# A 4-bit FFN kernel: dequantization scales repeated over partitions by transfers, not by expander matmuls

## What is computed

```python
def dequant4bit(q, scale):                      # BLOCK = 64
    return (q.astype(jnp.float32) - 7.5) * jnp.repeat(scale, BLOCK, axis=1)
...
q_emb = relu(cond @ W3 + b3)                    # one vector per batch
v = (64 * x + sum over the 64 rows of x) * q_emb
x1 = relu(v @ W2 + b2)
w_up = dequant4bit(w_up_q, w_up_scale).T        # 512 x 2048
x2 = relu(x1 @ w_up + b_up + x1 @ w_up_lora_a @ w_up_lora_b)
w_down = dequant4bit(w_down_q, w_down_scale).T  # 2048 x 512
out = x + x2 @ w_down + b_down + x2 @ w_down_lora_a @ w_down_lora_b
```

## Time and profile before

| | us |
|---|---|
| median of 3 runs | 833.25 (833.24 to 834.16) |
| span of the profiled execution | 832.3 |
| PE busy | 811.9 (98%) |
| DVE busy | 302.3 (36%) |
| ACT busy | 239.4 (29%) |
| POOL busy | 21.4 (3%) |

### The profile page before, as it was taken

The page is one execution under the profiler, slowest core; times in us unless marked ns, Lnnn a source line. Parts: engine busy times, 40 slices in busy tenths (PEclk is TensorE's granted clock), DMA queues, the critical chain, the costliest instruction groups (busy, mean ns, idle before and its releaser), DMA issues.

```text
span 832.3 us, 9143 instructions
## 1 busy us (share of the span) xinstructions
PE 811.9 (98%) x3576; PEld 671.5 (81%) x3576; DVE 302.3 (36%) x450; ACT 239.4 (29%) x370; POOL 21.4 (3%) x16
## 2 busy tenths in 40 slices
PE   5799999999999999999999999999999999999998
PEld 4578888888888888888888888888888888888886
DVE  6888885322132331423223132332224222241111
ACT  3353442422232222322214222232223322132221
POOL 3411000000000000000000000000000000000000
PEclk9799999999999999999999999999999999999999
DMA  8910001500004000120004000040000300020001
GB/s 318 419 50 1 1 0 52 151 1 1 0 1 152 0 0 0 55 97 0 0 0 148 3 0 0 0 151 0 0 0 31 120 0 0 0 100 2 1 1 51
DMA packets 13697, 39.64 MB, mean 48 GB/s; under 512 B 1648, under 2 KB 1776, under 8 KB 11760
## 3 DMA queue, kind: packets, MB, share of 16 engines
q1 hardware_dynamic: 13392, 39.33, 13.5%
q10 hardware_dynamic: 288, 0.08, 0.0%
HBM read 31.01 MB, written 8.39 MB: 47 GB/s over the span
## 4 chain that ended last, share of the span: by engine, by line
PE 95%; DVE 4%; DMA 1%; issue 0%; ACT 0%; DVEq 0%; ACTq 0%
PE up_ps L488 15%; PE up_ps L489 15%; PE up_ps L490 15%; PE acc L488 14%; PE acc L489 14%; PE acc L490 14%; PE lora_ps L488 1%; PE scale_ps L488 1%; PE lora_ps L490 1%; PE scale_ps L490 1%; PE lora_ps L489 1%; PE scale_ps L489 1%; DMA biases<-in_biases 1%; DVE x_in L389 1%; DVE xm_lo L399 1%; DVE xm_hi L397 0%
## 5 line engine op out<-in xcount | busy, mean ns | idle before, releaser
L405 DVE TENSOR_TENSOR x_lo<-full,x_hi 128x512 fp32r<-128x512 f32 x160 | 110.5, 691 | 469.8 <-ACT x_hi L271 469.8
L269 ACT ACTIVATE full<-up_ps,biases 128x512 f32<-128x512 f32 x142 | 97.9, 689 | 508.9 <-PE up_ps L490 508.9
L488 PE MATMUL up_ps<-x_hi,w_up_hi 128*128 128x512 f32 x512 | 200.2, 391 | 0.7 <-DVE x_lo L405 0.7
L489 PE MATMUL up_ps<-x_lo,w_up_hi 128*128 128x512 f32 x512 | 200.1, 391 | 0.0
L490 PE MATMUL up_ps<-x_hi,w_up_lo 128*128 128x512 f32 x512 | 199.7, 390 | 0.0
L490 PE MATMUL acc<-x_hi,w_down_lo 128*128 128x512 f32 x512 | 199.2, 389 | 0.0
L489 PE MATMUL acc<-x_lo,w_down_hi 128*128 128x512 f32 x512 | 199.2, 389 | 0.0
L488 PE MATMUL acc<-x_hi,w_down_hi 128*128 128x512 f32 x512 | 199.2, 389 | 0.0
L488 PEld LDWEIGHTS up_ps<-x_hi,w_up_hi 128*128 128x128 f32 x512 | 96.4, 188 | 20.7 <-DVE x_lo L405 0.9
L490 PEld LDWEIGHTS up_ps<-x_hi,w_up_lo 128*128 128x128 f32 x512 | 96.5, 188 | 20.1
L489 PEld LDWEIGHTS up_ps<-x_lo,w_up_hi 128*128 128x128 f32 x512 | 96.6, 189 | 19.6
(11 more groups left out here) (68 smaller groups left out, 401.4 us busy)
## 6 DMA issues: line engine op xcount, KB each, us to landing
x_in<-in_x SPq DMA_DIRECT2D x32, 256.0 KB, 5.7
res<-in_x SPq DMA_DIRECT2D x8, 1024.0 KB, 6.8
out<-res SPq DMA_DIRECT2D x32, 256.0 KB, 2.7
codes_up<-in_q_up SPq DMA_DIRECT2D x3, 1024.0 KB, 18.7
codes_down<-in_q_down SPq DMA_DIRECT2D x3, 1024.0 KB, 21.1
raw_records<-in_records SPq DMA_DIRECT2D x3, 768.0 KB, 18.1
raw_w<-in_w SPq DMA_DIRECT2D x4, 256.0 KB, 7.9
raw_narrow<-in_narrow SPq DMA_DIRECT2D x1, 1024.0 KB, 11.4
```

The costliest lines, as they stand in the source:

```text
L269: act.activation(whole, source, ACT.Relu, bias=bias_col).then_inc(relu_done, 1)
L405: dve.tensor_tensor(lo, full[:, slot % FULL_SLOTS, :], hi.bitcast(F32), ALU.subtract).then_inc(act_split, 1)
L488: pe.matmul(dest, w_hi, a_hi, start=start, stop=False)
L489: pe.matmul(dest, w_hi, a_lo, start=False, stop=False)
```

## The change

The scales are no longer expanded by TensorE. A tile of 128 partitions (inputs) spans two groups of 64 inputs, so the host lays each table out as two rows of 16 x 512 elements (`s_up`, `s_down`), and SP loads each row with a source repeated over 64 partitions: `scale[0:64]` from row 0, `scale[64:128]` from row 1. For each of the five groups there are now six transfers: codes and two scale copies for up, and the same for down; the semaphore of the group is waited for at 96. The scale tables have the size of the codes and lie where the low parts go; the codes now lie where the high parts go.

`dequantize` reads codes and scales from SBUF and writes over the scales; the LoRA product is added in place, and `weight_high` and `weight_low` read from there. The scratch and the wait for it go. `expand` has one product left, into two banks `lora_ps` in turn. Of `records` only the LoRA part is left (`wide`, 16 x 128 per partition); it is loaded in one transfer, cast by one ACT copy, and split by one POOL instruction on 64 partitions, ahead of the last w2 tile's low part. `narrow` has two parts in place of four. The five record casts, the five record splits and the split of `scale_down` go. In front of group 0's loads stand narrow, wide and the last w2 tile.

The diff, cut to its core:

```diff
-        narrow_r = sb("narrow", [P, 3, D], F32R)
-        lora_up, scale_down, lora_down = narrow_r[:, 0, :], narrow_r[:, 1, :], narrow_r[:, 2, :]
-
-        codes_up = sb("codes_up", [P, NH, D], I32, over="w_up_lo")
-        codes_down = sb("codes_down", [P, NH, D], I32, over="w_down_lo")
-
-
-
-        REC = 3 * P
-        REC_SKIP = 4 * NH * (D - REC)
-        raw_narrow = sb("raw_narrow", [P, 4, D], F32, over="w_up_hi")
-        raw_records = sb("raw_records", [P, NH, REC], F32, over="w_up_hi", skip=REC_SKIP)
-        record = sb("record", [P, NH, REC], F32R, over="w_down_hi", skip=REC_SKIP)
-        raw_w2 = sb("raw_w2", [P, KD, D], F32, over="w_down_hi")
-        assert 4 * 4 * D <= REC_SKIP
-        weight = sb("weight", [P, 2, D], F32, over="res")
-        expand_up = sb("expand_up", [P, D], F32R, over="res", skip=2 * 4 * D)
+        narrow_r = sb("narrow", [P, 2, D], F32R)
+        lora_up, lora_down = narrow_r[:, 0, :], narrow_r[:, 1, :]
+        wide = sb("wide", [P, NH, P], F32R, over="res")
+
+        codes_up = sb("codes_up", [P, NH, D], I32, over="w_up_hi")
+        codes_down = sb("codes_down", [P, NH, D], I32, over="w_down_hi")
+
+        scale_up = sb("scale_up", [P, NH, D], F32, over="w_up_lo")
+        scale_down = sb("scale_down", [P, NH, D], F32, over="w_down_lo")
+        raw_wide = sb("raw_wide", [P, NH, P], F32, over="x1_hi")
+        raw_w2 = sb("raw_w2", [P, KD, D], F32, over="x1_lo")
+        raw_narrow = sb("raw_narrow", [P, 2, D], F32, over="x2_lo", skip=1024)
...
-        scale_ps = ctx.enter_context(nc.psum_tensor("scale_ps", [P, BANK], F32))
-        lora_ps = ctx.enter_context(nc.psum_tensor("lora_ps", [P, BANK], F32))
-        w2_ps = [up_ps[0], up_ps[1], scale_ps, lora_ps]
+        lora_ps = [ctx.enter_context(nc.psum_tensor(f"lora_ps{m}", [P, BANK], F32)) for m in range(2)]
+        w2_ps = up_ps + lora_ps
...
-        def scratch(e):
-            return like(e, weight[:, e % 2, :])
+        def whole(e):
+
+            return part_of(e, scale_up4, scale_down)
...
-            def load_group(g):
-                a, b = GROUPS[g]
-                sp.dma_start(raw_records[:, a:b, :], records[:, a:b, :]).then_inc(record_loaded[g], 16)
-
             def load_codes(g):
                 a, b = GROUPS[g]
-                sp.dma_start(codes_up[:, a:b, :], q_up[:, a:b, :]).then_inc(codes_loaded[g], 16)
-                sp.dma_start(codes_down[:, a:b, :], q_down[:, a:b, :]).then_inc(codes_loaded[g], 16)
+                for codes, q, scale, s in ((codes_up, q_up, scale_up, s_up), (codes_down, q_down, scale_down, s_down)):
+                    sp.dma_start(codes[:, a:b, :], q[:, a:b, :]).then_inc(codes_loaded[g], 16)
+                    for half in range(2):
+                        rows = slice(half * P // 2, (half + 1) * P // 2)
+                        sp.dma_start(scale[rows, a:b, :], s[half:half + 1, a:b, :].to_broadcast([P // 2, b - a, D])).then_inc(
+                            codes_loaded[g], 16)
...
-            sp.dma_start(raw_narrow[:], narrow[:]).then_inc(narrow_loaded, 16)
-            load_group(0)
+            sp.dma_start(raw_narrow[:], narrow[:]).then_inc(tables_loaded, 16)
+            sp.dma_start(raw_wide[:], wide_in[:]).then_inc(tables_loaded, 16)
             sp.dma_start(raw_w2[:, KD - 1, :], w2[:, KD - 1, :]).then_inc(w2_loaded[KD - 1], 16)
-            load_codes(0)
-            for g in range(1, len(GROUPS)):
-                load_group(g)
+            for g in range(len(GROUPS)):
                 load_codes(g)
...
-                act.copy(part_of(e, w_up_hi, w_down_hi), scratch(e)).then_inc(weight_hi, 1)
-
-            def cast_records(g):
-                a, b = GROUPS[g]
-                act.wait_ge(record_loaded[g], 16)
-                act.copy(record[:, a:b, :], raw_records[:, a:b, :]).then_inc(record_cast, 1)
+                act.copy(part_of(e, w_up_hi, w_down_hi), whole(e)).then_inc(weight_hi, 1)
...
-            act.wait_ge(narrow_loaded, 16)
-            act.copy(expand_up[:], raw_narrow[:, 0, :]).then_inc(narrow_cast, 1)
-            act.copy(lora_up, raw_narrow[:, 1, :]).then_inc(narrow_cast, 1)
-            cast_records(0)
+            act.wait_ge(tables_loaded, 32)
+            act.copy(lora_up, raw_narrow[:, 0, :]).then_inc(table_cast, 1)
+            act.copy(wide[:], raw_wide[:]).then_inc(table_cast, 1)
             act.wait_ge(w2_loaded[KD - 1], 16)
             act.copy(w2_hi[:, KD - 1, :], raw_w2[:, KD - 1, :]).then_inc(w2_cast, 1)
-            act.copy(narrow_r[:, 1:3, :], raw_narrow[:, 2:4, :]).then_inc(narrow_cast, 1)
-            cast_records(1)
...
+            pool.wait_ge(table_cast, 2)
+            pool.tensor_tensor(wide[2 * QUAD:P], raw_wide[2 * QUAD:P], wide[2 * QUAD:P].bitcast(F32),
+                               ALU.subtract).then_inc(table_split, 1)
+            pool.wait_ge(table_split, 1)
             low_of_w2(KD - 1)
             pool.wait_ge(w2_split, KD)
-            pool.wait_ge(narrow_cast, 3)
-            pool.tensor_tensor(scale_down[2 * QUAD:P, :], raw_narrow[2 * QUAD:P, 2, :],
-                               scale_down[2 * QUAD:P, :].bitcast(F32), ALU.subtract).then_inc(scale_down_split, 1)
-            pool.wait_ge(scale_down_split, 1)
...
-                group = records_needed(e) - 1
-                if e == 0 or group != records_needed(e - 1) - 1:
-                    dve.wait_ge(codes_loaded[group], 32)
-                dve.wait_ge(scale_ready, e + 1)
-                if e >= 2:
-                    dve.wait_ge(weight_ready, e - 1)
-                dve.scalar_tensor_tensor(out=scratch(e), in0=part_of(e, codes_up4, codes_down), scalar=-ZERO_POINT,
-                                         in1=like(e, scale_ps), op0=ALU.add, op1=ALU.mult).then_inc(dequant_done, 1)
+                group = group_of(e)
+                if e == 0 or group != group_of(e - 1):
+                    dve.wait_ge(codes_loaded[group], 96)
+                dve.scalar_tensor_tensor(out=whole(e), in0=part_of(e, codes_up4, codes_down), scalar=-ZERO_POINT,
+                                         in1=whole(e), op0=ALU.add, op1=ALU.mult).then_inc(dequant_done, 1)
                 dve.wait_ge(dequant_done, e + 1)
                 dve.wait_ge(lora_ready, e + 1)
-                dve.tensor_tensor(scratch(e), scratch(e), like(e, lora_ps), ALU.add).then_inc(weight_full, 1)
+                dve.tensor_tensor(whole(e), whole(e), like(e, lora_ps[e % 2]), ALU.add).then_inc(weight_full, 1)
...
+                if e == 0:
+                    pe.wait_ge(table_split, 1)
                 if CHUNKS[e] == (DOWN, 0):
-                    pe.wait_ge(scale_down_split, 1)
-                    pe.wait_ge(lora_down_split, 2)
-                count = 1 + (form == PAIR)
-                rows = record[:, t, 0:P]
-                scale_up, wide = (record[:, t:t + count, i * P:(i + 1) * P] for i in (1, 2))
-                for bank, still, moving, still_down, moving_down, freed, made in (
-                        (scale_ps, expand_up, scale_up, rows, scale_down, dequant_done, scale_ready),
-                        (lora_ps, lora_up, wide, record[:, t, 2 * P:3 * P], lora_down, weight_full, lora_ready)):
-                    if e >= 1:
-                        pe.wait_ge(freed, e)
-                    if form == DOWN:
-                        mm = pe.matmul(bank[:], still_down, moving_down, start=True, stop=True)
-                    else:
-                        ks = range(KD) if form == ONE else range(2 * CHUNKS[e][2], 2 * CHUNKS[e][2] + 2)
-                        dest = bank[:].rearrange("p (t k h) -> p t k h", t=count, h=P)
-                        for n, k in enumerate(ks):
-                            mm = pe.matmul(dest[:, :, n, :], still[:, k * P:(k + 1) * P], moving, start=True, stop=True)
-                    mm.then_inc(made, 1)
+                    pe.wait_ge(table_split, 3)
+                if e >= 2:
+                    pe.wait_ge(weight_full, e - 1)
+                bank = lora_ps[e % 2]
+                if form == DOWN:
+                    mm = pe.matmul(bank[:], wide[:, t, :], lora_down, start=True, stop=True)
+                else:
+                    count = 1 + (form == PAIR)
+                    ks = range(KD) if form == ONE else range(2 * CHUNKS[e][2], 2 * CHUNKS[e][2] + 2)
+                    dest = bank[:].rearrange("p (t k h) -> p t k h", t=count, h=P)
+                    for n, k in enumerate(ks):
+                        mm = pe.matmul(dest[:, :, n, :], lora_up[:, k * P:(k + 1) * P], wide[:, t:t + count, :], start=True, stop=True)
+                mm.then_inc(lora_ready, 1)
...
+        "s_up": a["ffn_w_up_scale"].reshape(nh, P, kd, 2).transpose(3, 0, 2, 1).reshape(2, nh, d),
+        "s_down": a["ffn_w_down_scale"].reshape(d, nh, 2).transpose(2, 1, 0),
```

(27 more changed lines are left out.)

36 lines of the change are left out of this document (9 added, 27 removed).

## The result

| | before | after |
|---|---|---|
| median of 4 runs, us | 833.33 (833.24 to 834.16) | 860.68 (860.11 to 862.24) |
| span of the profiled execution, us | 832.3 | 860.2 |

The ratio is 1.0327 (95% interval 1.0312 to 1.0342): 27.4 us slower. The forecast was 839.5, slower by 6.2, with a range up to 842.5; the sign was right, the size was not, and the time lies where rival D stood.

A forecast was written before the change was run, and what follows sets the result against it. TensorE was taken to bound the kernel; -6.7 matmuls, -1.4 bank, 0 start, +0.6 VectorE, +14.1 late x, less 0.3 counted twice, gave +6.3 on 832.3, plus 0.95 to the median: 839.5 us, range 824.5 to 842.5.

The forecast's parts named there:

- rival D: Scale loads: reading one HBM row 64 times is itself slow; at 3 times, x lands at 99, about 860 us; chance 0.12.
- Matmuls removed: TensorE: 29 chunks behind the start each lose a scale expansion of 0.23 us, a gain of 6.7 us.
- the bank: Second LoRA product bank: the expansion behind up 1 starts without waiting for VectorE, a gain of 1.4 us.
- VectorE's pace: VectorE becomes slower than TensorE by 0.7 us per two pairs; after its lead is spent, 0.6 us of waits.
- the start: Loads and splits ahead of the first chunks: later restart offset by earlier chunk 1; taken as 0, ends -1 and +2 us.
- the end named as -1: Lower end for the start: TensorE's clock comes back one stretch earlier, 1 us gained.
- The scale copies' own rate: Copies on 64 partitions run at half rate, since no partition was seen taking in more than 3.3 GB/s.
- 8 MiB cost 8/0.403 = 19.9 us more: SP's queue: half-rate scale copies delay block 1's x by 19.9 us, to 79.1, 14.1 us after VectorE wants it.
- The estimate of +10 us: Alternative sum using the Trainium skill's 196 GB/s for 64 partitions: scales take 2.2 times as long, about +10 us.
- break-even: Block 1's x may land at 72.5, reached when scale copies take 1.67 times as long as full-width ones.
- SP's time: Sixteen more transfers in SP's queue at 0.33 to 0.43 us each, some 6 us, less than SP's idle time before x's issue.
- B: Transfers run at full rate or below 1.35 times, x arrives before VectorE wants it: 825.8 us; chance 0.29.

The follow-up runs named there:

- full_copies: Changed kernel, but scale tables repeated to 128 rows in HBM by the host and each group's scales loaded in one transfer on all 128 partitions; 826.72 us, ratio 0.9912.
- codes_then_middle: Changed kernel with host-repeated scale tables, all code loads first, then scales in sweeps over partitions 32-95, 0-31, 96-127; 861.64 us, one run.

## Why the prediction was wrong, and where it was right

**Matmuls removed, the bank, VectorE's pace, the start: right as a sum, with two misses in it that cancel.** The prediction's sum without the transfers was -7.5 us, and full_copies, which is that case, measured -7.5 (826.72 against 834.22; the profiled spans differ by 8.0). The matmuls and the bank came as forecast: from the end of up 0 to the start of up 2 TensorE gains 2.06 us on the kernel before, and 0.23 for each later expansion. The start was to be worth nothing and gave 1.1. VectorE's lag was to cost 0.6 and cost 1.1, lost between 93 and 118 us; the prediction's own terms, 3 us of lag less 2.0 of lead, make 1.0. Of the parts by full_copies' trace: the first x tile of block 1 was to land at 59.2 and landed at 59.1. VectorE was to want it at 65.0; line 339 ran at 64.07. VectorE was to need 12.6 us for two pairs; it took 76.69 - 64.07 = 12.62:

```profile
64.07 0.68 DVE L339 TENSOR_REDUCE sums<-x_in 128x8 f32<-128x512 f32 x1
...
76.69 0.68 DVE L339 TENSOR_REDUCE sums<-x_in 128x8 f32<-128x512 f32 x1
```

```profile
38.00:40.00 2.00, 0.73 (x3) 0.65 (x4) 2.00 (x5) 0.95 (x2) 0.00 (x0) 1.00 0.99 414
60.00:110.00 50.00, 49.82 (x225) 40.54 (x224) 43.26 (x69) 19.63 (x32) 0.00 (x0) 1.00 0.00 1
```

TensorE stands idle for 50 - 49.82 = 0.2 us in this stretch by the row, but the same products, laid side by side, show the 1.1: its lead over the kernel before is 1.07 at the end of up 0 (42.12 against 43.19) and 8.03 at 123.71, where 1.07 + 1.37 for the bank + 29 x 0.23 make 9.1. As for the start, GpSimd's low part was put at about 4.5 us, where its two rows make 4.2; it took 4.54 in the changed kernel and 5.07 in full_copies. The last split came at 31.5 as walked (TensorE restarts at 31.65), but the clock stayed up in 38 to 40 us (1.00, against 0.72 in the earlier trace rows), and up 0 ended at 42.12, not 43.2. That is the gain that lay at the end named as -1, the clock back one stretch earlier; why it came so here the runs do not show, and that it and VectorE's lag cancel is luck. The changed kernel itself does not have it: the wide table landed at 19.7, not at 17.8 as in full_copies, although it stands ahead of every scale copy in the queue; the restart came at 32.3, and up 0 ended at 44.2 after a stretch at half clock.

**The scale copies' own rate: right, by a wrong reason.** They were taken at half of the full-width rate; one-sided sweeps measured 204 to 213 of 423 GB/s. The reason given, that no partition takes in more than 3.3 GB/s, was refuted by codes_then_middle (6.6 GB/s into each of 64 partitions). It was an absence of rows read as a bound: every load of the kernel before writes all partitions, so it could not tell a limit of the partition from one of the side.

**The failed step: "8 MiB cost 8/0.403 = 19.9 us more".** It slowed the scales and left the codes between them at full rate. The two together were slower than that: 16 MiB at some 215 GB/s (0.205 MiB/us) take 78 us, against 40 at full rate. x landed at 99.9, 40.8 us later than in full_copies; the prediction had 19.9 and 79.1. Of the 40.8, 15 to 20 are the scales' own rate (238 to 211 GB/s), and the other 21 to 25 come of the two kinds in one queue. The estimate of +10 us that stands beside the sum leaves them out too. The sum had 14.1 us of wait for x; VectorE waited 23.1, and it came to that point 12.7 us late (76.8, against 64.07 in full_copies), because group 2 was late first: foreseen at 47.9 against a want of 48.9, the narrowest of the groups, it came at 60.5 and cost VectorE 10.6 us. With both waits TensorE idled 28.2 us, and the half clock behind each stall, which the prediction hid under VectorE's lag, cost 2.4 and about 2.9 us, and 1.4 more at up 0: 28.2 + 6.7 = 34.9 of the 35.9 us between full_copies' span and the changed kernel's. The prediction's break-even, copies 1.67 times as long, was in terms of the scales alone; counted over the 16 MiB in the queue, a landing 13.3 us later means 53 in place of 40 us, a rate of 317 GB/s; the measured 215 is far below. SP's time was mis-sized as well, at 0.33 to 0.43 us for a transfer: a copy of scale_up or scale_down held SP for 0.47 to 4.5 us, and x was issued at 55.0. That is no further cost, since the transfer engines were busy all the while (DMA share 0.98 to 1.02 in the rows above).

**The rivals.** B is full_copies, to within 1 us. D was priced at 860, with x at 99, and given 0.12 for a source read 64 times; that mechanism is worth nothing, and that its price is the time measured is luck. What D described in effect, the loads three times as long, is what the narrow transfers and their neighbours did together: by the rate over both kinds, 8 MiB of scales were charged 58 us (78 less 20 for the codes), 2.9 times their 20. The range ended at 842.5 because two costs in one place, narrow copies and slowed neighbours, were never added.

## What to carry to other kernels

What counted for these loads is whether a transfer touches partitions on both sides of number 64, not how many: fill both halves in one transfer, from a source with more copies in HBM if need be (34 us here, for 8 MiB). A repeated source row is no reason against it; one transfer that repeats each of two rows 64 times was not tried. Charge a slow transfer for the whole queue, its full-width neighbours and whatever stands last in it, and ask who waits for that last one. A rate that no row shows is no bound; price the case in which the neighbours suffer too.

## What the runs showed of the hardware

- One-sided transfers move at 204 to 213 GB/s, two-sided ones at 411 to 424; lower and upper halves in turn at 225 to 250; 64 neighbouring partitions from 32 to 95 are two-sided, and every second partition is too.
- A source row read 128 times over from HBM moves as fast (420 GB/s) as 128 different rows.
- Full-width loads that alternate with one-sided ones: 208 to 222 GB/s over both, where the two rates by themselves would give 282 to 305; 245 with half as many changes.
- The 16 parts of one transfer of 256 KiB ended up to 4.0 us apart in a queue of two-sided loads, and up to 8.2 us apart in the mixed one.
- Each of the two stalls of TensorE of over 8 us was followed by 5 to 6 us at half clock. Whether up 0, behind a wait of about 2 us, ran at full clock differed between kernels with the same TensorE program, and was worth 1 to 2 us.
